# A fused transformer block on one core: the opening and the eight images in one block, without the barrier between them

## The chip, the core and the metric

The kernel runs on one core of a Trainium2 chip. The core has five engines that run their own instruction streams and meet at semaphores: TensorE (PE: matmuls and transposes; its weight loads are listed as PEld), VectorE (DVE), ScalarE (ACT), GpSimd (POOL) and SyncE (SP, which here only issues DMAs). The metric is the device time of one launch in microseconds (us), the median of the runs.

## What is computed

Eight images of 1024 tokens and 256 channels go through one adaLN block: a modulation from a small vector, an attention with compressed keys and rotary parts, and a mixture of 16 small experts per head, of which two are used.

```python
mod = (silu(c) @ wmod).reshape(8, 6, 1, 256)
sa, ca, ga, sb, cb, gb = mod[:, 0], mod[:, 1], mod[:, 2], mod[:, 3], mod[:, 4], mod[:, 5]
ga = (2 * (ga >= 0) - 1) * maximum(abs(ga), 0.25)      # and gb the same way
h = layernorm(x) * (1 + ca) + sa
# attention: 16 heads, content width 16 and rotary width 32, causal over 1024 tokens
kv_c = rmsnorm(h @ W_kv) * g_kv;  q_c = h @ W_q
k_content, v, q_content = heads(kv_c @ W_kdec), heads(kv_c @ W_vdec), heads(q_c @ W_qdec)
k_rope, q_rope = rope(heads(h @ W_krope)), rope(heads(q_c @ W_qrope))
attn = softmax(causal(concat(q_content, q_rope) @ concat(k_content, k_rope).T / sqrt(48)))
x = x + ga * (attn @ v) @ W_o
# experts: tokens of 8 heads x 32, 16 experts, the two likeliest are summed
h = layernorm(x) * (1 + cb) + sb
t = (h @ Wm + bm).reshape(-1, 32)
w = softmax(t @ expert_emb);  topw, topi = top_k(w, 2)
eo = gelu(t @ W1[e] + b1[e]) @ W2[e] + b2[e]
x = x + gb * ((sum of topw * eo[topi]) @ Wo + bo)
```

## The kernel before

The program has two blocks. `opening` (L878) loads the weights, computes the modulation of all images and does the first image's projections and a part of its row maxima. Behind it every engine meets at a barrier, before which GpSimd clears all named semaphores; `all_images` (L1193) then runs the eight images.

**Heads and maxima.** The 16 heads stand in four groups of four (g = 0 to 3). Before the scores of a group are exponentiated, the maximum of every query row must be known. `item_matmuls` (L418) computes the scores of a pair of heads once only for their maxima ("pair" items: two matmuls, read on DVE by L558 where the causal mask is needed, by L561 where not), a "row" item transposes the maxima of a group and a half c (L487, copied by L569) and a DMA (L761, `move_row`) puts them as an extra row under the queries in q2[g]. The scores proper (L1236) then come out with the maximum subtracted. Query rows 0 to 511 are c = 0 and need 8 pairs (PAIRS[0]: 16 reads on DVE), rows 512 to 1023 are c = 1 and need 16 pairs (PAIRS[1]: 32 reads).

**Slots.** `attend_slots` places all of this by hand in 48 slots per image. A slot is one (g, c, j) of `MAIN`: (0,0) takes slots 0 to 3, (1,0) 4 to 7, (0,1) 8 to 15, (2,0) 16 to 19, (3,0) 20 to 23, and so on. In each slot TensorE does the first half of the scores, the items "between", the second half, the items "behind" and "front", and in every second slot the products with the values (L1256). ScalarE exponentiates (L1338) and GpSimd applies the causal select (L1446). The items share three PSUM banks in turn, 6, 7 and 5 (`Ring`, `ring_write`): a matmul waits until the read three places back is done. The opening uses five banks, 3 to 7. TensorE executes in program order, so an item that waits holds the scores behind it.

**Ropes.** Rotary projections are items "rope" 0 to 15: matmuls (L464 for keys, L466 for queries), two operations on DVE (L590, L591), two on GpSimd (L708, L720), and after two of them four DMAs (L746, `move_rope`). Ropes 8 to 15 belong to groups 2 and 3 and are done in the first image's attention slots.

**SP's queue.** SP issues its DMAs in program order and waits in that order too: content of the heads (L753, `move_content`), the row of minus ones under the keys (L767, `move_neg`), ropes, rows of maxima, and in `load_rows` the image (L1500), columns and gates of the modulation. Groups 2 and 3 lie in the region "wide", in which the opening also keeps the two halves w1h and w1l of the first expert weights until they are copied to w1s (L944 to L947).

The opening's end on each engine: TensorE does the last 4 of 6 modulation matmul groups (L1001), the 8 pairs of (0,0), a row, the 8 pairs of (1,0), a row and 4 pairs of (0,1) (`EARLY = 4`). DVE reads them and between them does six small operations on the gates (L1043 to L1052). ScalarE copies the modulation (L993) and rounds w1 (L995), GpSimd subtracts (L982), SP copies the four pieces of w1s and waits for all that is under way.

## Time and profile before

| what | value |
|---|---|
| median of 3 runs | 2950.63 us (2949.89 to 2953.15) |
| span of the profiled execution, first to last instruction | 2947.5 us |
| TensorE, busy share of the span | 96% |
| VectorE | 63% |
| ScalarE | 61% |
| GpSimd | 42% |
| mean granted clock of TensorE | 0.991 |
| share of TensorE in the chain that ended last | 85% |

The profile names instructions by line, engine and operation with the tiles that they write and read, and says for every idle stretch of an engine which instruction ended it. A granted clock of 1.00 is TensorE's level of 2.4 GHz and 0.50 its level of 1.2 GHz; a stretch in between has parts at both. Over the whole span TensorE is full. The first 90 us are the exception: by the page's slices they are the only ones with a busy share of 6 to 8 tenths.

### The profile page before, as it was taken

The numbers are of one execution on the slowest core, as the hardware profiler recorded it, in microseconds if no ns is written. First come the engines' busy times: TensorE is split into PE (matmuls) and PEld (weight loads), VectorE is DVE, ScalarE is ACT, GpSimd is POOL, SyncE is SP. The second block draws the span as 40 slices with busy tenths as digits, with TensorE's granted clock in tenths as the row PEclk, the third lists the DMA queues.
The fourth block names the chain that finished last, engine by engine and source line by source line (L and its number), as shares of the span: only waits on it lengthen the run. The fifth ranks groups of instructions, "written<-read, shape, count | busy, mean of one in ns | idle before, by whom it ended". The sixth has DMA issues, their size and how long they took to land.

```text
span 2947.5 us, 51530 instructions
## 1 busy us (share of the span) xinstructions
PE 2823.2 (96%) x16460; PEld 1254.0 (43%) x16460; DVE 1869.7 (63%) x4636; ACT 1806.7 (61%) x2148; POOL 1243.5 (42%) x1325
## 2 busy tenths in 40 slices
PE   6789999999999999999999999999999999999999
PEld 2344444444444444444434444444444444444433
DVE  5665766756667566666666666675756657666553
ACT  1346675566755667456674576655766566655687
POOL 4311555126551364413644146531465225661254
PEclk9889999999999999999999999999999999999999
DMA  6303443034430444204432044321553124531243
GB/s 141 73 1 84 113 121 96 4 98 112 133 73 2 106 123 118 70 8 119 121 100 70 21 128 122 90 56 29 134 130 91 34 63 115 130 84 27 74 129 93
DMA packets 177556, 253.06 MB, mean 86 GB/s; under 512 B 51085, under 2 KB 83869, under 8 KB 177197
## 3 DMA queue, kind: packets, MB, share of 16 engines
q1 hardware_dynamic: 170300, 247.79, 32.9%
q10 hardware_dynamic: 6996, 1.99, 0.3%
q8 instruction: 140, 2.29, 0.3%
q14 instruction: 120, 0.98, 0.1%
HBM read 159.13 MB, written 12.63 MB: 58 GB/s over the span
## 4 chain that ended last, share of the span: by engine, by line
PE 85%; DVE 6%; issue 3%; ACT 2%; POOL 1%; SPq 0%; DMA 0%; ACTq 0%; DVEq 0%; POOLq 0%
PE ps L1236 17%; PE ps L1272 17%; PE ps L1290 16%; PE ps L1256 9%; PE ps L418 8%; PE ps L464 4%; PE ps L505 2%; PE ps L466 2%; PE ps L535 2%; DVE front L561 1%; PE ps L516 1%; DVE rest L1392 1%; PE ps L492 1%; PE ps L523 1%; PE ps L450 1%
## 5 line engine op out<-in xcount | busy, mean ns | idle before, releaser
L1356 ACT ACTIVATE rest<-ps 128x1024 f32<-128x1024 f32 x1024 | 993.7, 1024 | 341.2 <-PE ps L1272 341.1
L1338 ACT ACTIVATE rest<-ps 128x1024 f32<-128x1024 f32 (+3 forms) x768 | 608.6, 810 | 550.1 <-PE ps L1236 536.4
L1456 POOL TENSOR_TENSOR rest<-rest 128x512 f32<-128x512 f32 x478 | 631.9, 1322 | 560.6 <-DVE rest L1392 550.1
L1392 DVE SCALAR_TENSOR_TENSOR rest<-ps,b2c,wide 128x512 f32<-128x512 f32 x512 | 383.8, 750 | 490.4 <-PE ps L1290 460.7
L1272 PE MATMUL ps<-wide,w1s 98*128 98x512 f32 x2048 | 644.6, 434 | 11.5 <-ACT rest L1356 8.7
L1290 PE MATMUL ps<-rest,w2s 128*32 128x512 f32 x4096 | 546.1, 605 | 0.6 <-ACT rest L1356 0.6
L1446 POOL TENSOR_SCALAR_AFFINE_SELECT rest<-rest 128x256 f32<-128x256 f32 x512 | 204.3, 407 | 806.7 <-ACT rest L1338 803.6
L558 DVE CUSTOM_DVE_ANT_0 rest<-ps,maskd 128x256 f32<-128x256 f32 (+3 forms) x1024 | 458.7, 487 | 121.9 <-PE ps L418 114.6
L1236 PE MATMUL ps<-wide 49*128 49x512 f32 (+3 forms) x2304 | 485.7, 511 | 7.2 <-ACT rest L1338 6.1
L1272 PEld LDWEIGHTS ps<-wide,w1s 98*128 98x128 f32 x2048 | 346.0, 189 | 238.4 <-ACT rest L1356 109.4
L561 DVE TENSOR_REDUCE front<-ps 128x1 f32<-128x512 f32 x512 | 329.1, 685 | 103.7 <-PE ps L418 99.9
L418 PE MATMUL ps<-wide 48*128 48x512 f32 (+3 forms) x1152 | 299.8, 509 | 33.0 <-DVE front L558 17.1
L1256 PE MATMUL ps<-rest,front 128*32 128x512 f32 (+3 forms) x3072 | 291.2, 497 | 0.0
L1236 PEld LDWEIGHTS ps<-wide 49*128 49x128 f32 x2304 | 196.4, 187 | 177.5 <-issue 110.4
L418 PEld LDWEIGHTS ps<-wide 48*128 48x128 f32 x1152 | 118.9, 187 | 294.2 <-issue 263.9
L708 POOL TENSOR_TENSOR front<-front,sin 128x512 f32<-128x512 f32 x128 | 163.6, 1278 | 89.8 <-DVE front L590 89.8
L1236 PE MATMUL ps<-heads 49*128 49x512 f32 (+3 forms) x768 | 166.4, 519 | 7.6 <-PEq L187 7.6
L720 POOL TENSOR_TENSOR front<-front 128x512 f32<-128x512 f32 x128 | 162.6, 1270 | 10.1
L1290 PEld LDWEIGHTS ps<-rest,w2s 128*32 128x32 f32 x4096 | 80.6, 108 | 191.2 <-issue 189.7
L1256 PEld LDWEIGHTS ps<-rest,front 128*32 128x32 f32 x3072 | 80.7, 110 | 155.0 <-issue 107.1
L464 PE MATMUL ps<-front,wkr 128*128 128x512 f32 x256 | 123.8, 611 | 0.0
L418 PEld LDWEIGHTS ps<-heads 48*128 48x128 f32 x384 | 36.9, 186 | 155.1 <-issue 149.6
(138 smaller groups left out, 2225.0 us busy)
## 6 DMA issues: line engine op xcount, KB each, us to landing
wide<-gate_rows SPq DMA_DIRECT2D x1024, 128.0 KB, 2.8
wide<-front SPq DMA_DIRECT2D x480, 64.0 KB, 2.0
wide<-front SPq DMA_DIRECT2D x192, 128.0 KB, 2.4
ao<-in_x SPq DMA_DIRECT2D x16, 512.0 KB, 5.0
heads<-front SPq DMA_DIRECT2D x64, 128.0 KB, 2.4
xs<-in_x SPq DMA_DIRECT2D x16, 512.0 KB, 5.1
out<-xs SPq DMA_DIRECT2D x32, 256.0 KB, 2.7
wide<-ao SPq DMA_DIRECT2D x96, 64.0 KB, 2.3
```

What stands on the lines that cost most here:

```text
L418: pe.matmul(outs[hh][:, 0:keys.stop - keys.start], L.q2[g][rows, pr, i * P:(i + 1) * P].bitcast(F32R), L.k2[g][rows, pr, keys].bitcast(F32 ...
L464: mm = pe.matmul(out, L.wkr[:, k, hd], L.ht[:, k, half(c)], start=(k == 0), stop=(k == CH - 1))
L558: v.tensor_tensor_reduce(out=R.junk[hh][:, 0:w], in0=src[:, 0:w], in1=L.maskd[:, HALF - w:], scale=1.0, scalar=-3e38, op0=ALU.add, op1=ALU ...
L561: v.tensor_reduce(dst, src[:, 0:w], AX.X, ALU.max).then_inc(read, 1)
L1236: mm = pe.matmul(bank(2 * (u % 2) + hh)[:, 0:HALF - f], L.k2[g][rows, pr, j * P:(j + 1) * P], L.q2[g][rows, pr, c * HALF + f:(c + 1) * HAL ...
L1256: mm = pe.matmul(bank(PVB)[h * VW:(h + 1) * VW, f:HALF], L.va[:, j, HG * g + h, :], L.pt[:, u % PTS, h % 2, f:HALF], start=(j == 0), stop= ...
L1272: mm = pe.matmul(bank(2 * (u % 2) + k), L.w1s[:, e, :], L.x2[:, c, 4 * j + 2 * p + k, :], start=True, stop=True)
L1290: mm = pe.matmul(bank(L2 + q % 2)[FD * h:FD * h + FD, :], L.w2s[:, e, :], L.hm[:, (2 * q + h // 2) % HM, (h % 2) * HALF:(h % 2 + 1) * HALF ...
L1338: nc.scalar.activation(L.pt[:, u % PTS, :, f:HALF], L.ps[:, 2 * (u % 2):2 * (u % 2) + 2, 0:HALF - f], ACT.Exp, scale=SCALE).then_inc(S["c_ ...
L1356: nc.scalar.activation(L.hm[:, u % HM, :], bank(2 * (u % 2), 2), ACT.Gelu).then_inc(S["e_gelu"], 1)
L1392: v.scalar_tensor_tensor(out=dst, in0=bank(L2 + q % 2), scalar=L.b2c[:, e:e + 1], in1=L.gb[:, q // 2 % GB, q % 2, :], op0=ALU.add, op1=ALU ...
L1456: g.tensor_tensor(dst, dst, L.gy[:, k % GY, :], ALU.add).then_inc(S["e_add"], 1)
```

## The change

The opening and the images become one block. The function `opening` becomes the class `Opening`, whose methods each engine calls ahead of its images. What the barrier had guaranteed is now waited for at the first use. Around it the first image's order changes:

- The opening keeps the 8 pairs of (0,0), the row (0,0) and six pairs of (1,0). The last two pairs of (1,0), its row and all 16 pairs of (0,1) go into slots 0 to 5, four per slot at most. Ropes 8 to 15 move from slots 0, 2 to 8 to slots 3, 5 to 11. The 32 pairs of slots 8 to 20 are spread two or three per slot. From slot 21 on nothing changes.
- The modulation matmuls of banks 1 and 2 stand behind the pairs of (0,0). The six operations on the gates stand behind slot 10's items. Their results go to DRAM behind the last rope of group 3, ahead of `load_rows`.
- w1s and the embedding are now copied by DMAs of ScalarE's queue, ahead of its first exponential. TensorE waits for them in slot 36, DVE for the late weights in slot 22.
- SP copies the content of groups 2 and 3 in two parts, with the row (1,0) between; the part that lies over w1h and w1l waits for w1s. The row (0,1) stands behind the first rope of group 2 instead of the second.
- The 86 semaphore clears of GpSimd are gone. A small tile `rs` gets memory of its own, and so do the four modulation rows m25.

```diff
@@ build
-        opening(nc, L)
-        for names in (L.names_a, L.names_b):
-            clear(nc.gpsimd, names)
-        nc.all_engine_barrier()
-        all_images(nc, L)
+        all_images(nc, L, Opening(nc, L))
@@ Opening.scalar
+        act.wait_ge(e.s_wl, self.late_done)
+        nc.scalar.copy(self.w1h, self.w1t).then_inc(e.s_pw, 1)
+        act.wait_ge(e.s_c, 1)
+        for k in range(4):
+            act.dma_start(e.embd[FD * k:FD * k + FD, NE * k:NE * k + NE], e.emb).then_inc(e.s_wd, 16)
+        act.wait_ge(e.s_pp, 3)
+        nc.scalar.copy(self.m25.rearrange("b j c -> b (j c)"), e.bank(1, 2)[0:B, :]).then_inc(e.s_pm, 1)
+        act.wait_ge(e.s_pw, 2)
+        for src, a, b in ((self.w1h, 0, 32), (self.w1l, 32, 64), (self.w1h, 64, 97), (self.w1l, 97, 98)):
+            act.dma_start(e.w1s[a:b, :, :].bitcast(F32), src[a:b, :, :].bitcast(F32)).then_inc(e.s_ws, 16)
@@ Opening.tensor
+        for item in self.first:
+            item_matmuls(pe, e, R, item)
+        pe.wait_ge(e.s_w1, 16)
+        modulation(1)
+        for item in self.second[:1]:
+            item_matmuls(pe, e, R, item)
+        modulation(2)
+        for item in self.second[1:]:
+            item_matmuls(pe, e, R, item)
@@ attend_slots, first image
-EARLY = 4
+EARLY = 6
+        per_slot = ((0, 2), (1, 2), (2, 4), (3, 2), (4, 4), (5, 4), (8, 2), (9, 2), (10, 2), (11, 3), (12, 3), (13, 2), (14, 3), (15, 2),
+                    (16, 3), (17, 2), (18, 3), (19, 2), (20, 3))
...
+        slots[1][2].append(("row", 1, 0))
-    ropes = {s: ("rope", 8 + k) for k, s in enumerate((0, 2, 3, 4, 5, 6, 7, 8))}
+    ropes = {s: ("rope", 8 + k) for k, s in enumerate((0, 2, 3, 4, 5, 6, 7, 8) if img else (3, 5, 6, 7, 8, 9, 10, 11))}
@@ scores
+                elif u == 0:
+                    pe.wait_ge(L.s_pv, 1)
+                    pe.wait_ge(L.s_pm, 1)
@@ SP, first image
+            def first_heads_in():
+                O.R.wait(sp, L, ("qc", 1, 1))
+                O.R.wait(sp, L, ("kc", 1))
+                move_content(sp, L, 0, range(2 * HG, 3 * HG), S["p_c2"])
+                move_content(sp, L, 1, range(3 * HG, 4 * HG), S["p_c3"])
+                front_row(sp, L, RA[0], 1, 0)
+                move_neg(sp, L, 3, S["p_ng"])
+                sp.wait_ge(L.s_ws, 64)
+                move_content(sp, L, 1, range(2 * HG, 3 * HG), S["p_c2"])
+                move_content(sp, L, 0, range(3 * HG, 4 * HG), S["p_c3"])
+                move_neg(sp, L, 2, S["p_ng"])
...
-                        if img == 0 and (g, k) == (3, 0):
+                        if img == 0 and (g, k) == (2, 1):
                             front_row(sp, L, RA[0], 0, 1)
...
+                if img == 0:
+                    sp.wait_ge(L.s_pm, 7)
+                    sp.dma_start(L.mod_dram[:, 2:6, :], O.m25).then_inc(L.s_wm, 16)
+                    sp.wait_ge(L.s_wm, 32)
```

What TensorE does around the first scores, before (from the row (1,0) on; heads is the region of group 0, wide that of the other groups):

```order
L487 MATMUL ps<-ident,front 16x128
L418 MATMUL ps<-heads 128x512 x4
L418 MATMUL ps<-heads 128x128 x4
L922 UNCONDITIONAL_BRANCH
L1213 UNCONDITIONAL_BRANCH
L1236 MATMUL ps<-heads 128x512 x2
L418 MATMUL ps<-heads 128x512 x2
L1236 MATMUL ps<-heads 128x512 x2
```

and after, from the matmuls of bank 1 on (L988 is the modulation, L483 the row (0,0), L414 the pairs):

```order
L988 MATMUL ps<-rest 8x512 x2
L483 MATMUL ps<-ident,front 16x128
L988 MATMUL ps<-rest 8x512 x2
L414 MATMUL ps<-wide 128x128 x4
L414 MATMUL ps<-wide 128x256 x4
L414 MATMUL ps<-wide 128x384 x4
L1238 MATMUL ps<-heads 128x512 x2
L414 MATMUL ps<-wide 128x512 x2
L1238 MATMUL ps<-heads 128x512 x2
```

The first scores now stand behind the row (0,0) and six pairs of group 1, with no branch between.

SP's queue from the row (0,0) on, before:

```order
L761 DMA heads<-front 1x4x128 [waits f_v,s_c]
L761 DMA heads<-front 1x4x128 x3
L942 DMA embd<-in_emb 32x16 x4
L944 DMA w1s<-wide 32x2048 [waits s_pw]
L945 DMA w1s<-wide 32x2048
L946 DMA w1s<-wide 33x2048
L947 DMA w1s<-wide 1x16x128
L761 DMA wide<-front 1x4x128 [waits f_v]
L761 DMA wide<-front 1x4x128 x3
L950 DMA mod_rows<-rest 8x1024 [waits s_pm]
```

and after (L757 moves rows, L749 content, L763 the minus ones, L742 ropes):

```order
L757 DMA heads<-front 1x4x128 [waits f_v]
L757 DMA heads<-front 1x4x128 x3
L749 DMA wide<-ao 16x1024 [waits f_a]
L749 DMA wide<-ao 16x1024 x3
L749 DMA wide<-front 16x1024 x4
L757 DMA wide<-front 1x4x128 [waits c_rd]
L757 DMA wide<-front 1x4x128 x3
L763 DMA wide<-neg 1x16x128 x2
L749 DMA wide<-front 16x1024 [waits s_ws]
L749 DMA wide<-front 16x1024 x3
L749 DMA wide<-ao 16x1024 x4
L763 DMA wide<-neg 1x16x128 x2
```

The weights' copies left SP's queue, and the content of groups 2 and 3 follows the row (0,0) at once.

## Rows read from the trace of the kernel before

**Rows 1.** Timeline of TensorE: start, duration, instruction, idle time before and its releaser.

```profile
56.40 3.60 PE L1001 MATMUL ps<-rest 128*8 128x512 f32 x8
67.14 0.37 PE L487 MATMUL ps<-ident,front 128*16 128x128 f32 x1 [2.42 <-DVE front L558]
67.69 0.70 PE L418 MATMUL ps<-wide 48*128 48x128 f32 x4 [0.18 <-DMA wide<-front]
80.56 0.47 PE L418 MATMUL ps<-heads 48*128 48x128 f32 x2 [0.72 <-DVE front L561]
88.63 2.08 PE L1236 MATMUL ps<-heads 49*128 49x512 f32 x4 [7.60 <-PEq L187]
```

**Rows 2.** Timeline of DVE, 57 to 82 us.

```profile
57.13 0.67 DVE L591 TENSOR_TENSOR front<-ps,cos 128x512 f32<-128x512 f32 x1
60.29 0.29 DVE L558 CUSTOM_DVE_ANT_0 rest<-ps,maskd 128x128 f32<-128x128 f32 x1 [2.48 <-PE ps L418]
66.30 0.69 DVE L558 CUSTOM_DVE_ANT_0 rest<-ps,maskd 128x512 f32<-128x512 f32 x1
68.17 0.29 DVE L558 CUSTOM_DVE_ANT_0 rest<-ps,maskd 128x128 f32<-128x128 f32 x1 [0.34 <-PE ps L418]
69.90 0.42 DVE L558 CUSTOM_DVE_ANT_0 rest<-ps,maskd 128x256 f32<-128x256 f32 x1
72.50 0.69 DVE L558 CUSTOM_DVE_ANT_0 rest<-ps,maskd 128x512 f32<-128x512 f32 x1
75.79 0.27 DVE L1043 TENSOR_SCALAR rest<-rest 8x256 f32<-8x256 f32 x1
78.54 2.46 DVE L561 TENSOR_REDUCE front<-ps 128x1 f32<-128x512 f32 x4
```

**Rows 3.** Timeline of SP's queue: each row is a run of DMA issues.

```profile
63.41 2.48 SPq L746 DMA_DIRECT2D wide<-front  x4
72.38 0.57 SPq L944 DMA_DIRECT2D w1s<-wide  x1
74.53 1.21 SPq L947 DMA_DIRECT2D w1s<-wide  x1
117.43 2.52 SPq L761 DMA_DIRECT2D heads<-front  x4
```

**Rows 4.** DMA issues of 20 to 100 us: KB each, median us to landing.

```profile
wide<-front SPq DMA_DIRECT2D x8, 128.0 KB, 2.3
```

**Rows 5.** Timelines of GpSimd, ScalarE and ScalarE's DMA queue.

```profile
63.35 4.51 POOL L982 TENSOR_TENSOR wide<-xs,wide 98x2048 fp32r<-98x2048 f32 x1
88.59 1.28 ACT L1338 ACT_TABLE_LOAD   x1 [25.75 <-PEq L187]
15.29 7.51 ACTq L989 DMA_DIRECT2D bmc<-in_bm  x1
```

**Rows 6.** Later places on TensorE's timeline: starts of slots 8 and 21.

```profile
122.08 1.99 PE L1236 MATMUL ps<-heads 49*128 49x512 f32 x8
179.37 0.92 PE L1236 MATMUL ps<-wide 49*128 49x384 f32 x4
```

**Rows 7.** Windows: length, busy us (and count) of PE, PEld, DVE, ACT, POOL; clock, DMA.

```profile
66.00:92.00 26.00, 10.95 (x38) 5.64 (x38) 15.09 (x58) 2.31 (x2) 2.02 (x2) 0.50 0.24 51
88.60:122.10 33.50, 31.02 (x163) 13.31 (x163) 22.45 (x58) 12.86 (x18) 21.04 (x28) 0.93 0.33 65
122.10:179.40 57.30, 49.55 (x297) 22.04 (x296) 35.69 (x123) 22.38 (x28) 12.05 (x22) 0.85 0.16 42
147.80:164.30 16.50, 14.42 (x76) 6.42 (x75) 8.79 (x25) 4.28 (x7) 2.44 (x6) 0.60 0.00 1
```

**Rows 8.** Groups of TensorE's and DVE's rows in one slot each, same timeline.

```profile
103.53 1.98 PE L464 MATMUL ps<-front,wkr 128*128 128x512 f32 x4
93.14 1.12 PE L466 MATMUL ps<-front,wqr 128*128 128x512 f32 x2
97.69 2.63 DVE L561 TENSOR_REDUCE front<-ps 128x1 f32<-128x512 f32 x4 [0.30 <-PE ps L418]
```

More of the change, by code:

```diff
@@ L264, in place @@
         L.ot = self.take("rest", 2, HALF)
-        L.rs = self.take("rest", 2, 4, HG)
         self.begin("rest", REST_WORDS - 2 * HALF)
@@ L1092, in attend_slots @@
     assert len(places) == len(pairs)
-    ropes = {s: ("rope", 8 + k) for k, s in enumerate((0, 2, 3, 4, 5, 6, 7, 8))}
+    ropes = {s: ("rope", 8 + k) for k, s in enumerate((0, 2, 3, 4, 5, 6, 7, 8) if img else (3, 5, 6, 7, 8, 9, 10, 11))}
     for (s, part), pair in zip(places, pairs):
-        if img == 0 and slots[s][0]:
-            part = 1
         if part and img and s and s in ropes:
@@ L1202, in all_images @@
         eslots.append(expert_slots(img))
-        before = {5: ("e_gy", NQ), 6: RE[-1].last(6), 7: RE[-1].last(7)} if img else {}
+        before = {5: ("e_gy", NQ), 6: RE[-1].last(6), 7: RE[-1].last(7)} if img else {b: O.R.last(b) for b in (5, 6, 7)}
         RA.append(Ring([item for slot in aslots[img] for part in slot for item in part], (6, 7, 5), "c_rp",
-                       {"v": "c_rd", "a": "c_ra"}, 8, moved, L.junk_a, before, img == 0))
+                       {"v": "c_rd", "a": "c_ra"}, 8, moved, L.junk_a, before))
         RE.append(Ring([item for slot in eslots[img] for item in slot] + [("out", 2), ("out", 3)] * (img + 1 == B), (6, 7),
@@ L1225, in scores @@
                         pe.wait_ge(S["p_ng"], 64)
-                    elif img and c == 0:
+                    elif c == 0:
                         pe.wait_ge(S["f_ng"], 64)
@@ L1233, in scores @@
                     pe.wait_ge(S["e_gelu"], NU - 1 + u)
+                elif u == 0:
+                    pe.wait_ge(L.s_pv, 1)
+                    pe.wait_ge(L.s_pm, 1)
+                else:
+                    name, count = O.R.last(3)
+                    pe.wait_ge(S[name], count)
                 for hh in range(2):
@@ L1250, in values @@
                     RE[img - 1].wait(pe, L, ("v", 1))
+                elif N == 0:
+                    pe.wait_ge(S["f_one"], 2)
+                    O.R.wait(pe, L, ("v", 1))
+                    name, count = O.R.last(PVB)
+                    pe.wait_ge(S[name], count)
                 if j == 0 and SEQ.index((g, c)):
@@ L1293, in outer @@
                 mm.then_inc(S["e_l2"], 1)
+            O.tensor(pe)
             for img in range(B):
                 for s, (between, behind, front) in enumerate(aslots[img]):
+                    if img == 0 and s == 36:
+                        pe.wait_ge(L.s_wd, 64)
+                        pe.wait_ge(L.s_ws, 64)
+                        pe.wait_ge(L.s_wl, O.late_done)
                     scores(img, s, 0)
@@ L1401, in add_last @@
                 v.tensor_tensor(dst, dst, L.gy[:, k % GY, :], ALU.add).then_inc(S["e_add"], 1)
+            O.vector(v)
+            O.R.wait(v, L, O.second[-1])
             for img in range(B):
@@ L1530, in _ @@
                     move_neg(sp, L, g, S["p_ng"])
+                store(img - 1, 1, RA[img])
+            def first_heads_in():
[9 more added lines that the diff above has]
+                move_neg(sp, L, 2, S["p_ng"])
+            O.sync(sp)
+            for img in range(B):
                 if img:
-                    store(img - 1, 1, RA[img])
+                    heads_in(img)
+                else:
+                    first_heads_in()
                 for g in range(2, NG):
                     for k in range(2):
-                        if img == 0 and (g, k) == (3, 0):
+                        if img == 0 and (g, k) == (2, 1):
                             front_row(sp, L, RA[0], 0, 1)
```

338 lines of the change are left out of this document (158 added, 180 removed).

## The prediction

> **What bounds the kernel now.** I read the page's busy shares first: TensorE is full for 96% of the span, so over the whole kernel only what shortens its work or fills its idle time counts. The images behind the first are not touched. What is left is the beginning, so I read the timelines of the first 180 us. TensorE's last pair of the opening starts at 80.56 and its first scores at 88.63, with 7.6 us of idle between [rows 1]: the barrier, the wait for the last DMAs and the semaphore clears. But the idle time is only the smaller part. Between the row (0,0) at 67.14 and the barrier [rows 1] stand the 8 pairs of (1,0), the gates (75.79 to 78.54) and the first pairs of (0,1) [rows 2], none of which the first scores need. In that stretch TensorE is busy for 11 of 26 us, at a granted clock of 0.50, while DVE does 15 us of reads [rows 7]. That is DVE's work holding TensorE, and it has to be done later in either case. So two questions decide: when can the first scores start, and how much of the work moved behind them fits beside TensorE's own.
>
> **Term 1: the first scores start earlier.** They need the row (0,0), the scores' banks, the minus ones, and TensorE's arrival.
> - The modulation's 3.60 us ahead of the pairs [rows 1] go. DVE is free from its last rope at 57.8 (57.13 + 0.67) instead of starting its reads at 60.29 [rows 2]; the 16 reads took 60.29 to 67.0, so they end near 64.5. One modulation of 1.8 us (half of 3.60) stands ahead of the row on TensorE; it fits into TensorE's own wait there, which was 2.42 us [rows 1]. Row copied at about 65.1.
> - SP is busy with the last rope of group 1 until 65.9 [rows 3]. Four row DMAs take 2.5 us to issue [rows 3], the last of them at 67.8, and DMAs land 2.3 us after issue [rows 4]: 70.1.
> - TensorE waits for group 1's ropes as before: pairs from 67.69 [rows 1], since SP's moves don't change. The second modulation lies before that, at 65 to 67. Six pairs are 12 reads, 68.17 to 72.50 [rows 2]. Their last matmuls wait for the seventh read (69.90 + 0.35) in the ring of five banks and end at about 70.7, behind the row's landing. So the first scores start at **70.7**.
> - ScalarE must first issue w1s, when GpSimd is done at 67.9 (63.35 + 4.51) [rows 5]. The four issues took SP 3.4 us (72.38 to 75.7) [rows 3], then the table load of 1.28 [rows 5]: ready at 72.6. The scores are ready at 70.7 + 2.1 = 72.8, if still at half clock (2.08 [rows 1]). It just fits.
> Term 1 is 88.6 - 70.7 = **17.9 us** of gain. The semaphore clears lie inside the 7.6 us of idle and go with it.
>
> The Trainium skill, page DMA: Bandwidth & Descriptors, section Issuing engines are not separate DMA queues, says that issuing from several engines at once only saves the sequencer's time to initiate a DMA, which is usually small beside the DMA. The four issues of rows 3 took SP 3.4 us, longer than a landing of 2.3 [rows 4], so here that time is not small; by the page moving them would be worth nothing and a sum that credited it would be too large. Mine credits nothing for it, and agrees with the page so far.
>
> **Term 2: slots 0 to 7 take longer.** Moved behind the first scores are, on DVE: two pairs of (1,0) (4 reads of 512, 2.4 us: 16 reads of 6.7 less 12 of 4.3), the first four pairs of (0,1) (2.5 unmasked, 0.9 masked), the row 0.3 and, in slot 10, the gates 2.75: 8.8 us in all [rows 2]. TensorE gets 2.7 us of matmuls with them. Slots 0 to 5 on DVE are now 2.4 + 16 unmasked reads of 0.66 [rows 8] + 16 masked 6.7 + two ropes 2.6 + sums and row 0.9 = 23.1 us, and DVE also finishes two of the early reads' microseconds first; TensorE has 21 to 22 us at full clock. I laid the slots one behind the other, each read as soon as its matmul and each matmul as soon as its bank is free three reads back: 4.6 us for slot 0 (half clock), then 3.2, 5.5, 1.9, 5.9, 6.6, 5.4 and 2.4, together 35.5 against 33.5 before [rows 7]. The longest, slots 4 and 5, are DVE's 8 reads each plus a rope. **Loss 2.0 us.** Bounds: 0 if the clock recovers sooner than slot 0's end and the reads pack; 6 if the clock falls again in slots 2 to 5, where TensorE is busy only some 80%.
>
> **Term 3: the row (0,1) behind a rope on SP.** SP now waits for ropes 8 and 9 before it may issue this row. Rope 9 is in slot 5, its two GpSimd operations end near 101.1 in my layout, its four DMAs are issued by 103.6, the row's by 106.1, and the last lands at 107.8. Slot 8 would be reached at 106.2. **Loss 1.7 us**, bounds 0 and 3. Before, the row was issued at 117.43 and slot 8 began at 122.08 [rows 3, 6], nothing waiting.
>
> **Term 4: slots 8 to 20.** Four ropes stand here instead of one: a key rope takes 1.98 us on TensorE and a query rope half of it, 1.0 [rows 8], so 5.8 against 2.0: +3.8. (These were in slots 0 to 7; that is why term 2 is small although eight pairs came in.) DVE has about 40 us there instead of 33. Adding up the larger of TensorE's and DVE's work slot by slot gives 51.7 us for after and 48.3 for before; before really took 57.3 (122.10 to 179.40) at a clock of 0.85 [rows 7]. The missing 9.0 are DVE waits and the half clock that came with them: 147.8 to 164.3 ran at 0.60 [rows 7]. After, the reads of slots 14 and 15 are lighter (3.2 against 5.5 us), those of 16 to 20 are as heavy as before, and slot 10 has the gates. I take 8 of these 9 again: 59.7, a **loss of 2.4 us**; bounds are a gain of 1.5 (4 us of such time) and a loss of 6.
>
> From slot 21 on the order is the same; a dip of the clock more or less is 1 us either way. The last check is SP: it reaches `load_rows` some 13 us after slot 11, needed in slots 16 and 22, so I cost it nothing.
>
> **Sum.** -17.9 + 2.0 + 1.7 + 2.4 = -11.8. The span goes from 2947.5 to 2935.7. The median stood 3.1 above the span, and the table load and launch around it do not change: **2938.8 us**.
>
> **The rivals.**
> - *The clock stays up.* TensorE has more to do between 58 and 67 than before, so the fall to 0.50 of rows 7 may come late or be short, and the more even slots 14 to 20 may escape theirs. Then terms 2 and 4 are about 0 and -1.5, sum -17.7: 2933. For it: 88.6 to 122.1 ran at 0.93 with the restart from half clock in it [rows 7]. Against: DVE is denser now.
> - *The clock stays down.* Slots 0 to 7 at DVE's pace give TensorE gaps in almost every slot, and in 147.8 to 164.3 just such a stretch, busy 87%, ran at 0.60 [rows 7]. A second stretch like that in slots 0 to 7 costs its half: 16 us at 0.60 instead of full, about 6 us where TensorE has no slack, so terms 2 and 4 become 8 and 4, sum about -4: 2946. The Trainium skill has the rule on page TensorE: Matmul & The Clock Gate, section A second HAM failure mode: psum-queue depth-cycling: small idles between groups of matmuls make the clock swing and cost throughput. Rows 7 agree with it; no row shows it for slots 0 to 7.
> - *ScalarE's DMAs hold the first exponential.* Issues on its queue were as slow as 7.51 us for one [rows 5]. If the w1s issues take that long, the first exponential comes at 76.7 instead of 72.8, sum -8: 2943.
> - *SP turns the gain into a loss.* The one queue now carries, between slots 5 and 16, rope, row, three ropes, the modulation's write with a wait for its landing, the image's load and then row (2,0). Slot 16 needs that row. Each microsecond by which the queue is behind at slot 16 is one lost on TensorE; I see 1 to 3 us of slack. It ends slower than before only from 12 us behind on, for instance if the write of the gates is held by DVE reaching slot 10 late and two further groups' moves queue behind: 2953.
> - *It does not do what it says.* If something else than the row holds the first scores (w1s, say, or the modulation's copy), term 1 shrinks to the barrier's 7.6 us and the sum to about -2: 2949.
>
> **How the numbers follow.** Forecast (sum between -7 and -16) 0.55, clock up 0.20, clock down 0.10, ScalarE 0.06, slower 0.04, not as said 0.05. A measurement of this kernel can tell about 0.2%, 5.9 us, from no change. Faster by more: forecast and clock up whole, ScalarE whole and a third of clock down: 0.84. Within: two thirds of clock down and "not as said": 0.12. Slower: 0.04. The range reaches from the clock-up end (-19: 2931.5) to the clock-down middle (-6: 2944.5).
>
> **What would show each step.** First scores (line 1238) at 70 to 71 us and the first exponential by 73: term 1. Slot 8 at 107 to 109 with TensorE idle just ahead of it on a DMA into heads: terms 2 and 3. Slot 21 at 166 to 169: term 4; at 161 to 163 and a clock near 1.0 in its window, the first rival. A clock of 0.5 to 0.7 over most of 75 to 100 is the second; ScalarE's first exponential past 75 the third; TensorE waiting ahead of slot 16 for a DMA into wide the fourth. The forecast is wrong in kind if first scores start after 75 or the gain at slot 21 is gone at slot 47.

## The result and the profile after

After: 2960.45 us, median of 6 runs (2957.71 to 2968.28). The kernel before beside it: 2950.26 us, 6 runs (2947.39 to 2957.93). The ratio is 1.0038 [1.0024, 1.0052]. The change makes the kernel slower by 0.4%, about 10 us; forecast was 12 us faster.

Over the whole span nothing is to be seen: TensorE is busy for 96% as before. The time lies in the first image. ScalarE's first exponential of each slot (line 1352, before 1338) is a clock for it. The profiled execution of after was the longest of its six (span 2966.5), so I profiled the same kernel a second time (span 2962.2, below as e12). Both stand here against the one profile of before; "ahead" is by how much the slot comes earlier than before, in us:

| place | before | after | after, second profile | ahead, forecast | ahead, measured |
|---|---|---|---|---|---|
| slot 0 | 90.74 | 76.54 | 76.62 | 17.9 | 14.2 and 14.1 |
| slot 6 | 115.68 | 109.59 | 105.56 | | 6.1 and 10.1 |
| slot 8 | 123.25 | 118.33 | 115.36 | 14.2 | 4.9 and 7.9 |
| slot 10 | 131.41 | 126.50 | 123.53 | | 4.9 and 7.9 |
| slot 12 | 139.14 | 143.22 | 140.12 | | -4.1 and -1.0 |
| slot 21 | 180.33 | 187.31 | 177.64 | 11.8 | -7.0 and 2.7 |
| slot 36 | 236.72 | 252.05 | 249.48 | | -15.3 and -12.8 |
| slot 47 | 273.17 | 289.04 | 286.47 | 11.8 | -15.9 and -13.3 |

So most of the start was gained as meant, and more than that was lost again, mainly in three pieces: slots 0 to 6, slots 10 to 12, and slots 21 to 36, where the prediction had said that the order is the same. What lies behind slot 47 differs by 3.2 and 1.4 us. The spans of the profiles differ by 19.0 and 14.7 us, the medians of the runs by 10.

**The start.** TensorE's timeline of after, the rows that answer to [rows 1] (start, duration, instruction, idle time before and its releaser):

```profile
65.79 3.58 PE L988 MATMUL ps<-rest 128*8 128x512 f32 x4
69.30 0.38 PE L483 MATMUL ps<-ident,front 128*16 128x128 f32 x1
71.68 0.44 PE L414 MATMUL ps<-wide 48*128 48x128 f32 x4
75.16 1.13 PE L1238 MATMUL ps<-heads 49*128 49x512 f32 x4 [0.52 <-DMA heads<-front]
```

The 7.60 us of idle are gone. The scores now wait for the landing of the row (0,0), as forecast, but at 75.2 and not at 70.7. DVE's timeline, against [rows 2], says that its last rope is 3.4 us later than before (57.13 there), and that its reads end at 67.8 instead of the 64.5 forecast:

```profile
60.56 0.67 DVE L587 TENSOR_TENSOR front<-ps,cos 128x512 f32<-128x512 f32 x1
61.15 0.28 DVE L554 CUSTOM_DVE_ANT_0 rest<-ps,maskd 128x128 f32<-128x128 f32 x1
67.15 0.69 DVE L554 CUSTOM_DVE_ANT_0 rest<-ps,maskd 128x512 f32<-128x512 f32 x1
```

and GpSimd, ScalarE's queue, ScalarE and SP's queue, against [rows 3] and [rows 5], that all follow:

```profile
66.78 4.51 POOL L962 TENSOR_TENSOR wide<-xs,wide 98x2048 fp32r<-98x2048 f32 x1
71.79 3.42 ACTq L981 DMA_DIRECT2D w1s<-wide  x4
75.24 1.28 ACT L1352 ACT_TABLE_LOAD   x1 [2.45 <-issue]
70.03 2.55 SPq L757 DMA_DIRECT2D heads<-front  x4
```

The 3.4 us arise far ahead of the part that the change moves. DVE's first use of the modulation (tile moda) waits for its load; after, then before:

```profile
27.92 2.97 DVE L593 TENSOR_SCALAR front<-ps,moda 128x512 f32<-128x512 f32 x4 [5.83 <-DMA moda<-mod_rows]
25.42 2.97 DVE L597 TENSOR_SCALAR front<-ps,moda 128x512 f32<-128x512 f32 x4 [4.22 <-DMA moda<-mod_rows]
```

So 2.5 of the 3.4 us are a load that landed later. The other 0.9 lie between there and the last rope (32.6 us against 31.7). TensorE's clock may account for these, but not for the whole. e13, whose mean clock from 10 to 40 us is 0.66 as in after, has this row at 25.11 and its last rope at 58.00; e7, whose clock is given as 1.00 there, has them at 28.09 and 60.25. Of all fourteen profiles here, six have the row at 25.1 to 25.4 us (before, e1, e3, e5, e9, e13) and eight at 27.0 to 28.6, the second profile of after among them. The opening of e1 and e3 is that of after to the letter, so the late landing does not follow from the order of the program alone. Why the load lands late is not shown. (A clock of 1.00 that early is to be read with care: e9's first modulation group took 3.57 us at 6 us, in a window given as 1.00, and that is what a group took at 0.50 in the rows above.)

**Slots 0 to 6, 8 to 21, 21 to 36.** Three windows of after, in the columns of [rows 7]:

```profile
76.50:109.60 33.10, 27.30 (x127) 12.13 (x125) 23.65 (x66) 9.81 (x15) 8.59 (x15) 0.71 0.21 41
118.30:187.30 69.00, 60.54 (x304) 25.51 (x302) 43.21 (x137) 23.22 (x29) 19.72 (x28) 0.75 0.17 43
187.30:252.10 64.80, 52.45 (x332) 23.63 (x330) 41.48 (x117) 27.57 (x35) 6.91 (x15) 0.97 0.01 2
```

The first two have a clock of 0.71 and 0.75. The third is the telling one: nearly full clock (0.97, as in the same slots before), TensorE busy for 52.5 of 64.8 us, and 8.4 us longer than the same slots before, in which it was busy for 52.6. Its cause stands in two pairs of rows. TensorE in one of these slots, after, then before:

```profile
209.49 0.80 PE L414 MATMUL ps<-wide 48*128 48x512 f32 x2
211.16 0.50 PE L414 MATMUL ps<-wide 48*128 48x512 f32 x2 [0.87 <-DVE front L557]
```

```profile
199.62 0.81 PE L418 MATMUL ps<-wide 48*128 48x512 f32 x2
200.26 1.03 PE L1236 MATMUL ps<-wide 49*128 49x512 f32 x4
201.29 0.50 PE L418 MATMUL ps<-wide 48*128 48x512 f32 x2
```

Before, a half of the scores (L1236) stood between the two pairs of a slot. After, both stand between the halves. A pair writes two places, and two pairs need four of a ring of three, so the second pair waits for DVE to read the first matmul of the first. Both of a pair's waits stand ahead of its matmuls in `item_matmuls`, so the whole pair stands: 0.87 us here, and as the sums below show up to 0.9 in eight waits for unmasked reads and up to 1.7 in seven for masked ones. In the diff it is two lines that are missing: of `attend_slots` the change also took away

```diff
-        if img == 0 and slots[s][0]:
-            part = 1
```

which had sent every further pair of a slot behind the second half. The waits of the 16 slots added up (engine and line waited for, us, times, longest), after (187.3 to 252.1 us), then before (180.3 to 236.7):

```profile
PE ps L414 <- DVE front L557: 6.9, 8, 0.9
PE ps L414 <- DVE front L554: 5.4, 7, 1.7
```

```profile
PE ps L418 <- DVE front L561: 2.3, 5, 0.6
PE ps L418 <- DVE front L558: 0.8, 1, 0.8
```

12.3 us against 3.1: the 9.2 between them cover the stretch's 8.4.

**Slot 10, the gates.** The six operations on the gates stand on DVE behind slot 10's items, with the next pair's reads behind them. DVE, GpSimd, then TensorE:

```profile
130.93 1.02 DVE L1040 TENSOR_SCALAR rest<-rest 8x256 f32<-8x256 f32 x1
131.88 0.41 DVE L1041 TENSOR_SCALAR rest<-rest 8x512 f32<-8x512 f32 x1
132.32 1.64 DVE L1043 TENSOR_TENSOR rest<-rest 8x512 f32<-8x512 f32 x1
134.78 0.68 DVE L1048 SCALAR_TENSOR_TENSOR rest<-rest 8x512 f32<-8x512 f32 x1
```

```profile
130.53 1.28 POOL L704 TENSOR_TENSOR front<-front,sin 128x512 f32<-128x512 f32 x1 [2.10 <-DVE front L586]
131.89 1.53 POOL L716 TENSOR_TENSOR front<-front 128x512 f32<-128x512 f32 x1
```

```profile
132.00 0.69 PE L414 MATMUL ps<-wide 48*128 48x256 f32 x2
135.94 0.58 PE L414 MATMUL ps<-wide 48*128 48x256 f32 x2 [3.25 <-DVE front L554]
138.49 3.63 PE L460 MATMUL ps<-front,wkr 128*128 128x512 f32 x4
```

The chain takes 4.5 us (130.93 to 135.46) instead of the 2.75 of [rows 2], since two of its operations run beside GpSimd's rope: 1.02 us for the one that took 0.27 [rows 2], 1.64 for the one that took 0.68 before. TensorE stands for 3.25 us, and behind it the clock is at half: the key rope takes 3.63 against 1.98 [rows 8]. Slots 10 to 12 take 16.7 and 16.6 us in the two profiles, against 7.7. Not all of these 9 us are the gates': two ropes were moved into slots 10 and 11 as well, and e7 below, which has the ropes and no gates, takes 11.2; e11, which has set the ropes back and the gates apart, takes 7.0. So the ropes are about 3.5 of the 9 and the gates about 5.4.

### The profile page after: what moved, and what is told of

Its sections match the earlier page's. It is cut to its first block, busy times and chain, and to the rows that moved or that the text cites. A ratio compares the mean times of both kernels' runs of the same rounds, so it can differ in the third digit from the quotient of the medians.

```text
span 2966.5 us, 51418 instructions
## 1 busy us (share of the span) xinstructions
PE 2839.6 (96%) x16460; PEld 1258.3 (42%) x16460; DVE 1872.3 (63%) x4636; ACT 1807.8 (61%) x2148; POOL 1245.2 (42%) x1325
## 4 chain that ended last, share of the span: by engine, by line
PE 85%; DVE 6%; issue 3%; ACT 2%; DMA 1%; SPq 1%; POOL 1%; ACTq 0%; DVEq 0%; POOLq 0%
PE ps L1238 17%; PE ps L1280 17%; PE ps L1298 16%; PE ps L1264 9%; PE ps L414 8%; PE ps L460 4%; PE ps L462 2%; PE ps L501 2%; PE ps L531 2%; DVE front L557 1%; PE ps L512 1%; DVE rest L1407 1%; PE ps L488 1%; PE ps L519 1%; PE ps L446 1%
## 5 line engine op out<-in xcount | busy, mean ns | idle before, releaser
L1280 PE MATMUL ps<-wide,w1s 98*128 98x512 f32 x2048 | 645.1, 435 | 11.5 <-ACT rest L1370 8.7
L414 PE MATMUL ps<-wide 48*128 48x512 f32 (+3 forms) x1152 | 301.6, 512 | 44.0 <-DVE front L554 25.5
L414 PEld LDWEIGHTS ps<-wide 48*128 48x128 f32 x1152 | 118.9, 187 | 303.3 <-issue 275.7
L414 PEld LDWEIGHTS ps<-heads 48*128 48x128 f32 x384 | 37.2, 188 | 158.0 <-issue 145.8
```

What stands on the lines that cost most here:

```text
L414: pe.matmul(outs[hh][:, 0:keys.stop - keys.start], L.q2[g][rows, pr, i * P:(i + 1) * P].bitcast(F32R), L.k2[g][rows, pr, keys].bitcast(F32 ...
L1280: mm = pe.matmul(bank(2 * (u % 2) + k), L.w1s[:, e, :], L.x2[:, c, 4 * j + 2 * p + k, :], start=True, stop=True)
```

## The experiments

Of each kernel the ratio is to the kernel before, run beside it on the same chip (its medians there: 2953.12 for e1, e2, e3 and e5, 2953.33 for e6 to e9, 2953.61 for e10 and e11, 2954.08 for e12 and e13). Slot times are from the profiled execution, which is not the median one: that of e5 was 6 us above its kernel's median, those of e1, e3 and e10 were 4, 7 and 9 us below.

**Theory and rivals.** Theory: the missing placement rule and the gates cost what the two sets of rows say. Rivals: the reads that moved behind the first scores are too many wherever they stand; or the clock falls for other reasons and the waits are its symptom.

### The placement of the second pair: e1, e2 and e5

e1 gives the rule back to slots 21 and later, e2 to all slots, and e5 takes it away from the kernel before in slots 21 and later.

```diff
@@ e1 (e2: without "and s >= 21"), in after
     for (s, part), pair in zip(places, pairs):
+        if img == 0 and s >= 21 and slots[s][0]:
+            part = 1
@@ e5, in before
-        if img == 0 and slots[s][0]:
+        if img == 0 and s < 21 and slots[s][0]:
             part = 1
```

> The changed kernel, with one thing put back: in slots 21 to 36 of the first image the second pair of maxima stands behind the second half of the scores again, as in the kernel before. Theory A (two pairs in a row need four places of a ring of three, so TensorE stands 0.87 us for DVE's first read in each such slot): slots 21 to 36 take about 8 us less than the 64.8 us of the changed kernel and the time falls by about 8 us, to just about the kernel before (ratio 0.998 to 1.002). Rival B (those slots are slow because DVE and the clock are behind from the earlier slots): no change, ratio 1.003 to 1.005.

> The changed kernel with the old rule in all slots of the first image: only the first pair of a slot stands between the halves of the scores, every further one behind. Theory A: as the late slots alone, and 1 to 4 us more in slots 2, 4 and 5, where four pairs stand as two and two: ratio 0.996 to 1.000. If three pairs in a row behind cost as much as two between, no more than the late slots alone bring.

> The kernel before, with one thing of the change alone: in slots 21 to 36 of the first image both pairs stand between the halves of the scores. Theory A: 8 us slower than the kernel before, ratio 1.002 to 1.004. Rival B: no change.

Measured: e1 2948.64 us, 0.9985 [0.9972, 0.9997]; e2 2948.67, 0.9988 [0.9976, 1.0000]; e5 2967.77, 1.0051 [1.0033, 1.0068], more than the 1.002 to 1.004 expected. Slots 21 to 36 took 54.9 us in e1 and 54.75 in e2 (before 56.4, after 64.7 and 71.8), and 71.8 in e5. TensorE of e1, in a slot of the same form as above, does not wait:

```profile
198.06 0.81 PE L414 MATMUL ps<-wide 48*128 48x512 f32 x2
198.70 1.03 PE L1240 MATMUL ps<-wide 49*128 49x512 f32 x4
199.73 0.50 PE L414 MATMUL ps<-wide 48*128 48x512 f32 x2
```

What follows: the rule is worth about 12 us to after by the medians (2960.45 to 2948.64) and 16 by the ratios (1.0038 to 0.9985), and its absence costs the kernel before 15 (2953.12 to 2967.77), in both directions more than all that the change lost. The cost has two parts. One is waits, at any clock: five profiles lack the rule in these slots (after, e12, e3, e5, e10), and in each TensorE's waits for DVE add up to 12.3 or 12.4 us, against 3.3 to 3.6 in the nine that have it (transposes counted in). So the waits are no symptom of the clock. On top, the clock may fall: in the five it was 0.97, 0.86, 1.00, 0.86 and 1.00 over these slots, in the nine never under 0.97. The two at 0.86, e12 and e5, spent 71.8 us there with a stretch at 0.50, for e12:

```profile
210.00:220.00 10.00, 8.50 (x45) 3.21 (x41) 3.92 (x14) 3.20 (x5) 1.73 (x5) 0.69 0.00 1
220.00:230.00 10.00, 8.71 (x26) 4.94 (x26) 4.00 (x12) 2.44 (x3) 0.72 (x2) 0.50 0.01 2
```

The Trainium skill, page TensorE: Matmul & The Clock Gate, section A second HAM failure mode: psum-queue depth-cycling, describes such micro-idles between groups of matmuls that cycle through PSUM banks and the swing of the clock that they bring. Two of the five profiles agree, with idles of up to 1.7 us in nearly every slot and then 0.50; in the other three the same idles brought no such stretch (after has 3 us at half clock there, e3 and e10 none). Since e1 and e2 cycle through the same ring, at a clock of 1.00 and with times in these slots among the shortest, it is the idles and not the cycling that matter here.

e2 is no better than e1. In slots 0 to 5 the rule hardly helps where four pairs stand in a slot: they stand as one and three instead of two and two, and the three behind wait as the two did (slot 2 has the same waits of 0.53, 0.45 and 0.81 us in e2 and in after; slots 0 to 6 took 32.0 us in e2, 33.1 in after).

### The gates: e3, e6 and e7

e3 moves the six operations from slot 10 to slot 7 in after. e6 is e2 with one of them in each of slots 6 to 11. e7 is e2 without them, and SP's write of the modulation no longer waits for them (so e7 leaves out the added one, the signs and the lower bound of the gates, and its result is not the block's); it has their whole price.

```diff
@@ e3, in after
-                    if s == 10 and img == 0:
+                    if s == 7 and img == 0:
@@ e6, in e2
-                    if s == 10 and img == 0:
-                        O.modulated_gates(v)
+                    if s in range(6, 12) and img == 0:
+                        O.modulated_gates(v, s - 6)
```

> The changed kernel with the six small operations on the gates behind slot 7's items instead of slot 10's. Theory C (in slot 10 they stand ahead of the reads that the ring waits for, beside GpSimd's rope, cost TensorE a 3.3 us stall and a fall of the clock): slots 10 and 11 take some 5 us less than their 16.7 us, ratio 1.001 to 1.003. Rival: the stall moves with them and nothing is gained, ratio 1.003 to 1.005.

> The changed kernel with two edits: every further pair of a slot behind the second half of the scores (as in the run before with that rule in all slots), and the six operations on the gates one by one behind the items of slots 6 to 11. Theory C (the six in a row hold the reads that the ring waits for): slots 9 to 11 lose the stall of 3 us and the fall of the clock behind it, 5 us less than with the rule alone, ratio 0.996 to 0.998. Rival: the price is that of the work itself, a few tenths, ratio 0.998 to 0.9995.

> The same rule for the pairs, and the six operations on the gates left out altogether; the modulation is written as it came (so the gates' lower bound and signs, and the one added to the scale, are missing). It measures what the six operations cost at most. Theory C: slots 9 to 11 take about 11 us instead of 16 to 17, ratio 0.996 to 0.998, and splitting them comes within 1 us of it. Rival: no difference from the rule alone (0.9988), since the stall has another source, the ropes moved into slots 8 to 11.

Measured: e3 2964.5 us, 1.0040 [1.0026, 1.0053], no better than after, as the rival said. Slots 10 to 12 are shorter (11.2 us), but slots 8 to 9 take 9.7 against 4.6. The stall has moved with its cause, and so have the two long operations, again 1.02 and 1.64 us, and again beside a rope of GpSimd. DVE and TensorE of e3:

```profile
115.55 1.02 DVE L1040 TENSOR_SCALAR rest<-rest 8x256 f32<-8x256 f32 x1
116.93 1.64 DVE L1043 TENSOR_TENSOR rest<-rest 8x512 f32<-8x512 f32 x1
120.82 0.50 PE L414 MATMUL ps<-wide 48*128 48x512 f32 x2 [3.55 <-DVE front L557]
```

e6: 2943.36, 0.9971 [0.9962, 0.9981]; e7: 2939.98, 0.9960 [0.9948, 0.9972]. Slots 10 to 12 took 11.5 and 11.2 us, against 16.4 in e2. So the gates cost e2 about 8.7 us (2948.67 to 2939.98; the two intervals do not meet), three times the 2.75 at which I had costed their work. Setting them apart gives back 5.3 of it by the medians, but the intervals of e2 and e6 overlap by a little, as do those of e6 and e7, so the size of this part is less sure than the stretch itself: 16.4 to 11.5 us. The granted clock over slots 10 to 12 says the same: 0.79 to 0.80 in the five profiles with all six operations in slot 10, 1.00 in the others. Set apart they still cost something: slots 8 to 10 take 9.5 us in e6 and 8.2 in e7, with 1.1 us of waits for DVE against none, where one operation beside GpSimd took 1.16 us instead of 0.41 and another 1.41 instead of 0.68.

### How many pairs before the first scores: e8 and e10

e8 is e6 with all eight pairs of (1,0), the row (1,0) and four pairs of (0,1) ahead of the first scores, as in the kernel before, but with neither barrier nor gates there; slots 0 to 5 then get two pairs each, and SP waits for the row (1,0) as an item of the opening. e10 makes the same edit in after alone.

```diff
-        self.second = [("row", 0, 0)] + [("pair", 1, *p) for p in PAIRS[0][:EARLY]]
+        self.second = [("row", 0, 0)] + [("pair", 1, *p) for p in PAIRS[0]] + [("row", 1, 0)] + [("pair", 0, *p) for p in PAIRS[1][:4]]
-        per_slot = ((0, 2), (1, 2), (2, 4), (3, 2), (4, 4), (5, 4), (8, 2), ...
+        per_slot = ((0, 2), (1, 2), (2, 2), (3, 2), (4, 2), (5, 2), (8, 2), ...
...
-        pairs = [("pair", 1, *p) for p in PAIRS[0][EARLY:]] + [("pair", 0, *p) for p in PAIRS[1]]
+        pairs = [("pair", 0, *p) for p in PAIRS[1][4:]]
-        slots[1][2].append(("row", 1, 0))
```

> As the run with the gates one by one, and in addition the opening keeps all 8 pairs and the row of (1,0) and the first 4 pairs of (0,1) ahead of the first scores, as the kernel before does; slots 0 to 5 have two pairs each. The first exponential comes 5 to 6 us later than in the changed kernel. Theory D (in slots 0 to 5 DVE sets the pace, so work taken out of them is given back in full): slot 6 is reached at the same time or up to 3 us earlier, ratio 0.994 to 0.998. Rival (starting early is worth its microseconds): slot 6 comes 3 to 6 us later, ratio 0.999 to 1.001.

> The kernel after with one change: all eight pairs of (1,0), its row and four pairs of (0,1) stand ahead of the first scores, and slots 0 to 5 get two pairs each. Both pairs still stand between the score halves in slots 21 to 36, and the six gate operations still stand together behind slot 10. Theory, three separate causes that add up: first exponential some 6 us later than in after (82 to 83 us against 76.5), slot 6 all the same 5 to 7 us earlier (102 to 105 against 109.6), slots 10 to 12 as long as in after (16 to 17 us), slots 21 to 36 as long as in after (63 to 66 us), slot 47 near 283 and the median 2954 to 2957, ratio 1.001. Rival, the earlier start does not matter once later stalls stand, since VectorE catches up in them: slot 12 at 143 as in after, slot 47 at 288 and the median at 2960.

Measured: e8 2940.72 us, 0.9962 [0.9948, 0.9976]; e10 2960.45, 1.0016 [1.0003, 1.0029]. First exponentials of slot 0 and slot 6:

| kernel | slot 0 | slot 6 | between |
|---|---|---|---|
| before | 90.7 | 115.7 | 24.9 |
| after, both profiles | 76.5, 76.6 | 109.6, 105.6 | 33.1, 28.9 |
| e6 | 76.3 | 108.9 | 32.6 |
| e10 | 84.9 | 104.7 | 19.8 |
| e8 | 82.9 | 102.7 | 19.8 |

e8 and e10 start 6 to 8 us later than after and are 1 to 7 us earlier at slot 6. The window of these slots in e8, and TensorE's waits in it against those of after:

```profile
82.90:102.70 19.80, 18.38 (x114) 8.90 (x114) 16.13 (x42) 9.83 (x13) 7.53 (x15) 0.93 0.18 30
```

```profile
PE ps L414 <- DVE front L554: 0.8, 2, 0.5
PE ps L414 <- DVE front L557: 0.4, 1, 0.4
```

```profile
PE ps L414 <- DVE front L557: 3.3, 5, 0.9
PE ps L414 <- DVE front L554: 2.4, 5, 0.8
```

What follows: of the 14 us by which after is ahead at the first exponential, the last 6 to 8 are worth nothing by slot 6. The last six pairs that it takes out of the opening come back at the same price or a higher one behind the first scores, as waits (5.7 us against 1.2) and as lost clock (0.71 against 0.93; the seven profiles of after's early order have 0.71 to 0.88, e8 and e10 0.93 both). A part of these differences is the landing of the modulation's load, at 27.9 and 28.1 us in after, 27.0 in e8 and 28.6 in e10. The best case of after's early order is e1, with the load at 25.4: it reaches slot 6 at 104.6, no earlier than e8 and e10. In whole times this is worth little, as far as it can be told: e8 against e6 is 2.6 us with overlapping intervals, and e10 has the very median of after, with a lower ratio whose interval overlaps after's. My numbers for e10 held for slot 6 (102 to 105), slots 10 to 12 (17.0 us) and slots 21 to 36 (63.2), so the causes stand apart in one profile, whose slot 47 came at 277.0 and not at 283; for the whole the rival's 2960 held and not my 2954 to 2957. Four of its twelve runs took 2949.7 to 2954.2, eight 2959.0 to 2963.0, and the profile is of the first four. What the others lost, no trace of mine shows.

### The old order without the barrier, and the ropes: e9, e11, and e12 and e13 as second profiles

e9 is e8 with ropes and pairs back in the slots of the kernel before: on TensorE, of the whole change only the order of the modulation and the absence of the barrier are left in the first image. e11 is e8 with the ropes alone put back. The gates stay one by one in slots 6 to 11. e12 is after once more, e13 is e9 once more.

```diff
@@ e9 and e11, in e8
-enumerate((0, 2, 3, 4, 5, 6, 7, 8) if img else (3, 5, 6, 7, 8, 9, 10, 11))}
+enumerate((0, 2, 3, 4, 5, 6, 7, 8))}
@@ e9 as well
+        places = [(k // 2, 0) for k in range(12)] + [(9 + k // 3, 0) for k in range(8)]
+        places += [(12 + k // 3, 0) for k in range(8)] + [(15 + k * 6 // 16, 0) for k in range(16)]
+        places += [(21 + k // 2, 0) for k in range(32)]
...
```

> One block without the barrier, but all of the first image's slots in the order of the kernel before: early work as in the run before this one, ropes in slots 0 and 2 to 8, and the pairs of slots 9 to 20 in their old places; only the gates go one by one into slots 6 to 11. It prices the barrier alone. If it is worth what the trace of the kernel before shows (7.6 us of idle, the gates 2.8, the modulation 3.6 ahead of the pairs, less one of the two if they share a wait), the ratio is 0.995 to 0.997; if the slots give it back, 0.998 to 1.000.

> The kernel e8 with ropes 8 to 15 back in the slots of the kernel before (0, 2 to 8) and the pairs left where they are. Theory A, the place of the ropes is what made e9 reach slot 21 4 us earlier than e8 (167.3 against 171.4): slot 12 near 129 to 130, slot 21 near 167 to 168, median 2936 to 2938. Theory B, it was the places of the pairs of slots 8 to 20: slot 6 at 105 as in e9, slots 12 to 21 as long as in e8 (38.6 us), slot 21 at 171 or later, median 2940 to 2943. A third way, as e9: two groups of times, one near 2935 and one near 2948, if ropes in slots 0 to 8 beside the pairs let the clock fall in some executions.

> The kernel after, unchanged, profiled once more, since its profiled execution (2968.3 us) stood 8 us above its median. Theory: what the order does repeats and what the clock does not. Slots 21 to 36 take 63 to 66 us again and slots 10 to 12 16 to 17; the first exponential comes between 73 and 77 and slots 0 to 6 take 31 to 33; the 8 us lie in one or two dips of the granted clock in slots 12 to 30, so slot 47 comes near 281 to 283. Rival: the spread lies behind the first image, slot 47 comes at 289 again while the whole takes 2960.

> The kernel e9, unchanged, profiled once more, since its times fell into two groups (2933 to 2936 and 2947 to 2951) and the profile showed the lower. Theory: the same instructions in the same slots, but a stretch of half clock in slots 12 to 20, as the kernel before had at 147.8 to 164.3 us: slot 12 at 129 to 132, slot 21 near 178 to 182 instead of 167. Rival: the 15 us lie behind the first image: slot 21 at 167 to 169 again in an execution of 2948.

Measured: e9 2949.2 us, 0.9981 [0.9969, 0.9993], its twelve runs between 2933.26 and 2951.57; e13, the same kernel, 2944.08, 0.9961 [0.9942, 0.9980], 2934.98 to 2949.23. Together they leave open which of e9's two expected ranges holds: the old order without the barrier is worth 4 us by the one and 10 by the other. e11 2939.27, 0.9952 [0.9938, 0.9966], all six runs within 2938.53 to 2939.60. e12 2963.16, 1.0034 [1.0020, 1.0048], which repeats after.

The first profile of e9 (span 2931.5) and that of e13 (2947.2) are 15.7 us apart with the same instructions. Windows 140 to 150, 150 to 160 and 160 to 170 us, e9 and then e13:

```profile
140.00:150.00 10.00, 7.70 (x68) 3.89 (x62) 7.29 (x21) 3.50 (x6) 1.61 (x5) 1.00 0.00 1
150.00:160.00 10.00, 7.07 (x55) 3.48 (x51) 7.95 (x25) 3.38 (x6) 2.43 (x6) 1.00 0.01 2
160.00:170.00 10.00, 9.52 (x45) 4.32 (x46) 6.74 (x16) 4.25 (x5) 1.62 (x4) 0.66 0.00 0
```

```profile
140.00:150.00 10.00, 7.75 (x49) 3.42 (x48) 6.70 (x21) 1.96 (x4) 1.63 (x4) 0.82 0.09 25
150.00:160.00 10.00, 8.99 (x42) 3.99 (x41) 4.47 (x15) 4.25 (x5) 1.22 (x3) 0.50 0.01 2
160.00:170.00 10.00, 9.14 (x44) 4.50 (x44) 4.67 (x13) 1.50 (x4) 1.22 (x3) 0.50 0.00 1
```

Slot 0 came at 80.4 and 82.0, slot 12 at 129.2 and 132.3, slot 21 at 167.3 and 178.3 (expected 178 to 182), slot 47 at 258.6 and 269.5; behind it lie 2672.9 and 2677.7. So 11 of the 15.7 us are in the first image, 8 of them in slots 12 to 21: one stretch of half clock of 20 us instead of a short one. In this order TensorE has idle time at full clock around 140 to 160 us (busy 7.1 to 7.7 of 10), and the same program saw the clock fall during it in one execution and behind it in the other. What decides between the two is not shown. The kernel before has such a stretch at the same place of the same order, 147.8 to 164.3 at 0.60 [rows 7].

e12's slots 21 to 36 took 71.8 us, not the 63 to 66 expected, with the half clock shown above; slots 10 to 12 repeated (16.6), and slots 0 to 6 took 28.9 with a clock of 0.88 instead of 33.1 with 0.71. Slot 47 came at 286.5, between the 281 to 283 of the theory and the 289 of its rival. The theory holds for what repeats (waits, and where the clock is in danger), while my size for each stretch came from one execution and missed by up to 7 us.

e11 against e8: the ropes in slots 0 to 8 make slots 8 to 12 shorter (16.5 us against 20.2) and slots 0 to 8 longer (34.0 against 29.7); slot 21 comes at 172.9 against 171.4. So the place of the ropes is not what had brought e9's profile there at 167.3. Of the 5.6 us between e9 and e11 at slot 21, 4.5 stand already at slot 0 (80.4 against 85.0), of which 2.9 are the landing of the modulation's load (25.3 against 28.2). Theory B's numbers did not hold whole either: slot 6 came at 111.4, not 105. e11 has the lowest ratio of all kernels here, though its interval overlaps those of e6, e7, e8 and e13. Its times are also the closest together: they lie within 1.1 us, where before's beside it reach from 2944.25 to 2961.11.

## Why the prediction was wrong

**The failed step** is the sentence "From slot 21 on the order is the same", and with it "a dip of the clock more or less is 1 us either way". The order was not the same, the deleted rule of placement is an edit that the prediction never costed, and the part on the change above says "From slot 21 on nothing changes" too. That is 8.9 us in the first profile and 16.0 in the second, where the prediction had nothing. e1 shows it alone turning 1.0038 into 0.9985, e5 shows it on the kernel before. The order of the instructions would have told it: it has two L414 groups in a row in these slots. The second step that failed is term 4's price for slot 10, 2.75 us of work where the gates cost 8.7 in whole times. With the rule back and the gates out, e7 has the ratio 0.9960, which is also the forecast's (2938.8 to 2950.63). That is luck in part: its slots 0 to 8 took 41.5 us where the prediction had 37.2, its slots 8 to 21 took 55.2 where it had 59.7.

The working of the whole, in us (minus is gain; both profiles of after against the one of before):

| term | forecast | after | second profile |
|---|---|---|---|
| 1, start | -17.9 | -14.2 | -14.1 |
| 2 and 3, to slot 8 | +3.7 | +9.3 | +6.2 |
| 4, slots 8 to 21 | +2.4 | +11.9 | +5.2 |
| slots 21 to 47 | 0 | +8.9 | +16.0 |
| behind slot 47 | 0 | +3.2 | +1.4 |
| sum | -11.8 | +19.0 | +14.7 |

- **Term 1**: right in kind, 3.7 us too large in these profiles. The modulation's load landed 2.5 to 2.7 us later than in before's profile, which the prediction had taken over as it stood. In e1 and e3, where it landed at 25.4 and 25.2, the first exponential came at 73.37 and 73.86, near the 72.8 forecast. One modulation group took 3.58 us at half clock, not 1.8, and held the row on TensorE for 1.5 us. The first exponential at 76.5 looks like the third rival's 76.7, yet that mechanism is wrong: the four issues took the 3.4 us forecast, and ScalarE was late because GpSimd was (66.78 against 63.35). Scores and table load again ended together. By the row, moving w1s off SP did save SP 3.4 us; no run here tells whether that was worth anything.
- **Term 2**: laid out read by read at full clock behind slot 0, 35.5 us for slots 0 to 7. The largest miss that both profiles share is slot 2, the first with four pairs: 8.3 us and not 5.5. There the two pairs between the halves wait for the ring 0.53 and 0.45 us and the second pair behind them 0.81, and from 84 to 90 us the clock is at 0.50. The layout had the ring's waits, but full clock. The rest of the first profile's excess is half clock from 98 us on, which the second does not have. The bounds of 0 and 6 hold the second profile and not the first.
- **Term 3**: its size was about right, for slot 8's scores waited for the row's DMA as forecast: 0.26 us (at 117.15) and 1.30 in the two profiles, 1.4 to 1.6 in e1, e2, e7, e8 and e10, 0.8 in e3, none in e6, against 1.7 forecast (1.6 by its own times, 107.8 less 106.2). In e9 and e11, with the ropes in their old slots, there is no such wait.
- **Term 4**: its "slot 10 has the gates" counted work of 2.75 us. What mattered was that six operations in a row, beside GpSimd, hold one read for which the ring waits, and take longer than the ring's three places allow. Slots 10 to 12 lost 9 us, 5.4 of them to the gates. Without gates, e7's slots 8 to 21 took 55.2 us against before's 57.1, so the rest of the term would have been a gain of 1.9 and not a loss of 2.4.
- **The rivals.** "The clock stays down" happened in slots 0 to 6 of the first profile (0.71), in its size of some 8 us, not in the second (0.88). SP held TensorE only for term 3's wait: between 76 and 290 us its matmuls waited 0.3 and 1.3 us for DMAs. The fourth rival's sign, a wait for a DMA into wide ahead of slot 16, is in neither profile of after; e3 has it once, 1.66 us. Slower had 0.04 by that mechanism alone; the true one was not among the rivals.

## What to carry to other kernels

Compare the order of the instructions over the whole stretch in which the generating code changed, rule by rule, before saying that a part stays the same: a deleted two-line rule outweighed the whole aim of this change. Cost a step by whose wait it prolongs and not by its own time: a chain of small operations belongs where no ring of buffers runs past its places, or is set one by one between reads. And work that a slower engine must do in any case is not gained by starting the faster engine earlier: compare at the first place where both have done it (here slot 6), not at the first score.

## What the runs showed of the hardware

- A small DVE operation that started beside a GpSimd operation ended 0.1 to 0.6 us behind that one: 1.02 us instead of 0.27 and 1.64 instead of 0.68, both times equal in after and e3; 1.16 instead of 0.41 in e6. GpSimd's own took 1.53 instead of 1.27. But L1041 started at 131.88, level with GpSimd's next operation (131.89), and took its usual 0.41. The Trainium skill, page SBUF — State Buffer, section Who interferes with whom, says that a DVE instruction with two SBUF inputs contends with a GpSimd instruction that reads SBUF. L1043 has two inputs, and agrees. L1040 has one; the page names such a case only for DVE's two-port modes, and whether L1040 runs in one no row says outright. That the one-input operation of 8x512 takes 0.41 us and the two-input one of the same size 0.68, with GpSimd idle, would fit it.
- One stretch of one kernel, 150 to 160 us, ran at a clock of 1.00 in one execution and at 0.50 in another (e9, e13), and single profiles of this kernel differed by 15.7 us in span. One load at the start landed at 25.1 to 25.4 us or at 27.0 to 28.6 in kernels whose openings differ in nothing (e1 and e3 against after). With differences of 10 us to explain, a second profile tells more than a finer reading of the first.
